# A two-layer model in one program: the state-space loop's order of turn, output and tokens, and one of eight gates computed inside that loop

## The reference, cut to what matters

```
decay = exp(-exp(w)) * (0.5 + 0.5 * tf)          # per batch and channel
ek, ekv = exp(min(f, 30)), exp(min(f, 30)) * f
nf, df  = forward scans of ekv, ek; nb, db = backward scans
euk = exp(min(u + f, 30))
num = nf + nb - ekv + euk * f;  den = df + db - ek + euk
gate = sigmoid(x) * num / max(den, 1e-8) * (0.8 + 0.2 * tf)

x = x + attention(gate0(x))      # 16 heads, causal
x = x + ternary_ffn(gate1(x))
x = x + state_space(gate2(x))    # 64 heads of 8, state 128, chunks of 32
x = x + moe(gate3(x))            # 8 experts, top 2
```

## Time and profile before

| | us |
|---|---|
| median of 3 runs | 716.97 (716.85 to 722.58) |
| the profiled execution, its own time | 719.14 |
| its span | 717.3 |
| PE busy | 557.5 (78%) |
| DVE busy | 405.2 (56%) |
| ACT busy | 370.4 (52%) |
| POOL busy | 147.3 (21%) |

### The profile page before, as it was taken

The page is one execution under the profiler, slowest core; times in us unless marked ns, Lnnn a source line. Parts: engine busy times, 40 slices in busy tenths (PEclk is TensorE's granted clock), DMA queues, the critical chain, the costliest instruction groups (busy, mean ns, idle before and its releaser), DMA issues.

```text
span 717.3 us, 13912 instructions
## 1 busy us (share of the span) xinstructions
PE 557.5 (78%) x5668; PEld 403.4 (56%) x5668; DVE 405.2 (56%) x597; ACT 370.4 (52%) x791; POOL 147.3 (21%) x115
## 2 busy tenths in 40 slices
PE   0187868577967686668999999998639999999980
PEld 0044546454545571345564556666528999997560
DVE  5889998868899367883755545453461121111223
ACT  6986887457786615754557555644321222222212
POOL 1000000000000125841009555520010322322210
PEclk9995687785597999988999999998758999999996
DMA  9500000000000100000000000000049999889825
GB/s 354 163 1 1 1 1 1 1 0 1 1 1 1 30 1 1 0 1 1 1 3 2 2 3 2 3 2 2 31 164 383 422 419 379 307 329 339 309 124 190
DMA packets 18479, 71.38 MB, mean 100 GB/s; under 512 B 4848, under 2 KB 9968, under 8 KB 14704
## 3 DMA queue, kind: packets, MB, share of 16 engines
q1 hardware_dynamic: 15408, 64.20, 23.6%
q0 software_dynamic: 1920, 5.25, 2.0%
q10 hardware_dynamic: 1088, 1.05, 0.4%
HBM read 65.77 MB, written 4.72 MB: 98 GB/s over the span
## 4 chain that ended last, share of the span: by engine, by line
PE 56%; DVE 26%; ACT 10%; issue 4%; DMA 2%; POOL 1%; SPq 0%; ACTq 0%; DVEq 0%; POOLq 0%
PE PS L1416 41%; DVE nmx L1017 3%; DVE arena L930 3%; DVE arena L927 3%; PE PS L1891 2%; PE PS L1454 2%; PE PS L1960 2%; ACT arena L604 1%; PE PS L1667 1%; DVE A L949 1%; PE PS L1532 1%; ACT arena L764 1%; DVE arena L1121 1%; PE PS L1492 1%; DMA arena<-ypair 1%
## 5 line engine op out<-in xcount | busy, mean ns | idle before, releaser
L1416 PE MATMUL PS<-arena 128*128 128x128 f32 (+6 forms) x1376 | 162.1, 296 | 17.1 <-DVE arena L1121 10.1
L1416 PEld LDWEIGHTS PS<-arena 128*128 128x128 f32 (+4 forms) x1376 | 129.3, 167 | 43.0 <-issue 26.1
L604 ACT ACTIVATE arena<-PS,nmx 128x128 f32<-128x128 f32 (+1 forms) x128 | 52.1, 424 | 44.8 <-DVE nmx L1017 44.8
L1469 PE MATMUL PS<-ident,arena 128*128 128x128 f32 x192 | 37.6, 350 | 32.6 <-ACT arena L591 30.5
L1364 DVE TENSOR_TENSOR R<-arena,PS 128x128 f32<-128x128 f32 x16 | 4.6, 288 | 89.3 <-ACT arena L858 89.2
L1469 PEld LDWEIGHTS PS<-ident,arena 128*128 128x128 f32 x192 | 29.1, 181 | 40.4 <-ACT arena L604 25.7
L383 POOL TENSOR_SCALAR arena<-ident,gcol 128x128 f32<-128x128 f32 x4 | 2.4, 601 | 234.0 <-DMA gcol<-in_gcol 234.0
L443 POOL TENSOR_TENSOR arena<-arena 128x1024 f32<-128x1024 f32 x16 | 37.8, 2367 | 41.1 <-DVE arena L1203 33.1
L475 POOL DMA_INDIRECT ypair<-arena,oid x20 | 19.8, 988 | 122.5 <-ACT arena L864 122.5
L1416 PE MATMUL PS<-arena,R 128*128 128x256 f32 x192 | 44.2, 380 | 0.6 <-ACT arena L864 0.6
L1416 PEld LDWEIGHTS PS<-arena,R 128*128 128x128 f32 x192 | 35.2, 190 | 5.1 <-issue 1.0
(11 more groups left out here) (299 smaller groups left out, 1202.9 us busy)
## 6 DMA issues: line engine op xcount, KB each, us to landing
arena<-in_moe SPq DMA_DIRECT2D x23, 1408.0 KB, 6.6
arena<-in_moe SPq DMA_DIRECT2D x23, 768.0 KB
inproj<-in_inproj SPq DMA_DIRECT2D x1, 1344.0 KB, 10.5
arena<-in_fT SPq DMA_DIRECT2D x1, 1024.0 KB, 4.9
xT<-in_xT SPq DMA_DIRECT2D x1, 1024.0 KB, 5.4
R<-in_w1T SPq DMA_DIRECT2D x1, 1024.0 KB, 7.4
R<-in_w2T SPq DMA_DIRECT2D x1, 1024.0 KB, 9.4
R<-in_w3T SPq DMA_DIRECT2D x1, 1024.0 KB, 11.5
```

Source lines behind the costliest of these rows:

```text
L604: sc.activation(pr[u % 2][:, j, 0:n], PS[:, 2 * (u % 2) + j // 2, (j % 2) * 256:(j % 2) * 256 + n], ACT.Exp, bias=nmx[:, u % 2, j:j + 1], ...
L1416: last = mm(dst, l, r, start=(n == 0), stop=(n == len(pairs) - 1))
L1469: last = nc.tensor.transpose(PSB[:, 4 * HALF + c:4 * HALF + c + P], pr[u % 2][:, j, k * P:(k + 1) * P], ident[:])
```

## The change

Three things are changed together.

First, the eighth gate (i = 7, that is m = 3, c = 1, used by the experts' half 1) leaves the attention. FRAME becomes 6 and GATES 7, so that six gates fill the 36 pieces of the attention. The pieces of a gate are cut differently: a scan pair is no longer one piece. k = 1 is now the forward scan alone, and the new k = 7 and k = 8 are the fix of the ends and the backward scan. The pieces of a frame on DVE are now: close the denominator and forward scan of the numerator; backward scan of the numerator; close the numerator; Newton and result; forward scan of the next denominator; backward scan of the next denominator.

Second, the eighth gate is computed in four units t of 256 columns (one channel tile, one batch) inside the state-space loop. SP loads the unit's part of f again. ACT makes its inputs (`unit_inputs`, four instructions) after `by_chunk` of odd tiles and the reciprocal guess (`unit_guess`, three instructions) in even tiles. DVE runs `unit_out(t-1)` and `unit_den(t)` after `gated` in even tiles, and `unit_num(t)` and `unit_min(t+1)` in odd ones, so 7 or 8 instructions in each tile. The decay is now a broadcast column and not a matrix.

Third, the loop's order. On PE, `segments(i+1, 0)` and `(i+1, 1)` stand ahead of `state(i, 1)`, `turn(i-1)` comes right behind `state(i, 1)`, `output(i-1)` behind `state(i, 3)`, and `tokens(i+1)` right ahead of `within(i)`. ACT and DVE follow: `add_out(i-1)` now comes in DVE's turn i, one earlier than before.

```diff
@@ SP @@
-            sp.wait_ge(S["dve_R"], 8)
-            sp.wait_ge(S["act_euk"], 16)
+            sp.wait_ge(S["dve_R"], 7)
+            sp.wait_ge(S["act_euk"], 14)
...
+            sp.wait_ge(S["dve_num"], GATES)
+            for t in range(UNITS):
+                c, ct, n, cols = unit_of(t)
+                if t:
+                    sp.wait_ge(S["act_euk"], 2 * GATES + 3 * t)
+                load(uf[t % 2], a["fT"][:, c, cols], "f")
@@ ACT, attention @@
-                if k == 0 and i < 7:
-                    scaled_inputs(i + 1, 0)
-                if k == 4 and i < 7:
-                    scaled_inputs(i + 1, 1)
                 if k == 1:
                     reciprocal_guess(i)
-                if k == 2 and i < 7:
-                    decay(i + 1)
-                if k == 3 and i < 7:
-                    bonus(i + 1)
+                if i < GATES - 1:
+                    if k == 2:
+                        decay(i + 1)
+                    if k == 3:
+                        scaled_inputs(i + 1, 0)
+                        bonus(i + 1)
+                    if k == 4:
+                        scaled_inputs(i + 1, 1)
@@ ACT, loop @@
+            def unit_inputs(t):
...
+                done(sc.activation(uek, uek, ACT.Exp))
+                sc.activation(uxe, uek, ACT.Copy, scale=dq[:, 3, ct, n:n + 1]).then_inc(S["act_euk"], 1)
+                sc.activation(ufc, uf[t % 2], ACT.Copy, scale=cb[:, n:n + 1]).then_inc(S["act_euk"], 1)
+                sc.activation(ug, uf[t % 2], ACT.Exp, bias=wu[:, 3, 1, ct:ct + 1]).then_inc(S["act_euk"], 1)
...
             by_chunk(0)
+            unit_inputs(0)
             for i in range(NT):
-                state(i, 1)
                 if i + 1 < NT:
                     decays(i + 1, 0)
                     decays(i + 1, 1)
+                state(i, 1)
+                if i:
+                    turned(i - 1)
                 state(i, 2)
                 state(i, 3)
+                if i % 2 == 0:
+                    unit_guess(i // 2)
+                if i:
+                    inverse_root(i - 1)
...
-                if i:
-                    turned(i - 1)
-                    inverse_root(i - 1)
+                if i % 2 and i < NT - 1:
+                    unit_inputs(i // 2 + 1)
@@ DVE @@
-                for part in ((0,), (2,), (3,), (5, 6), ())[k]:
+                for part in ((0, 2), (8,), (3,), (5, 6), (), ())[k]:
                     gate_step(i, part)
...
-                if k == 4 and i < 7:
-                    gate_step(i + 1, 1)
+                if k >= 4 and i < GATES - 1:
+                    gate_step(i + 1, 1 if k == 4 else 7)
...
+            def unit_scan(t, x, y):
+                c, ct, n, cols = unit_of(t)
+                d = dec[:, 3, ct, n:n + 1].broadcast_to([P, T])
+                done(v.tensor_tensor_scan(y, d, x, 0.0, ALU.mult, ALU.add))
+                done(v.tensor_tensor(y[:, T - 1:T], y[:, T - 1:T], rdq[:, 3, ct, n:n + 1], ALU.mult))
+                done(v.tensor_tensor_scan(y[:, 0:T - 1][:, ::-1], d[:, 1:T], y[:, 0:T - 1][:, ::-1], y[:, T - 1:T], ALU.mult, ALU.add))
...
             for i in range(NT):
                 if i:
                     gated(i - 1)
-                if i >= 2:
-                    add_out(i - 2)
+                if i % 2 == 0:
+                    if i:
+                        unit_out(i // 2 - 1)
+                    unit_den(i // 2)
+                else:
+                    unit_num(i // 2)
+                    if i < NT - 1:
+                        unit_min(i // 2 + 1)
+                if i:
+                    add_out(i - 1)
                 if i + 1 < NT:
                     front(i + 1)
             gate(3, 0)
             gated(NT - 1)
-            add_out(NT - 2)
+            unit_out(UNITS - 1)
@@ PE, loop @@
             for i in range(NT):
-                state(i, 1)
                 if i + 1 < NT:
                     segments(i + 1, 0)
                     segments(i + 1, 1)
-                    tokens(i + 1)
+                state(i, 1)
+                if i:
+                    turn(i - 1)
                 state(i, 2)
                 state(i, 3)
+                if i:
+                    output(i - 1)
                 if i + 1 < NT:
                     segments(i + 1, 2)
                     segments(i + 1, 3)
                 if i % 2 == 0:
                     state(i, 4)
+                if i + 1 < NT:
+                    tokens(i + 1)
                 within(i)
-                if i:
-                    turn(i - 1)
                 between(i)
-                if i:
-                    output(i - 1)
@@ tables @@
-FRAME = 5
+FRAME = 6
+GATES = 7
+UNITS = 4
```

More of the change, by code:

```diff
@@ L138, in build, with unit_of @@
         wter = arena[:, 27 * K:30 * K].bitcast(BF).rearrange("p (w n) -> p w n", w=3)
+        uf = [ekvq[:, 512 + T * i:512 + T * (i + 1)] for i in range(2)]
+        uek, ufc, uxe, uxv = [dmats[0][:, T * i:T * (i + 1)] for i in range(4)]
+        ug, unf, udf, udb = [dmats[1][:, T * i:T * (i + 1)] for i in range(4)]
+        def unit_of(t):
+            c, ct, b = 1, t // 2, t % 2
+            n = 2 * c + b
+            return c, ct, n, slice(ct * HALF + b * T, ct * HALF + (b + 1) * T)
         def by_half(o):
@@ L973, in _ @@
             gate_step(0, 1)
+            gate_step(0, 7)
             gate_step(0, 0)
             gate_step(0, 2)
+            gate_step(0, 8)
             gate_step(0, 3)
@@ L982, in _ @@
             gate_step(1, 1)
+            gate_step(1, 7)
             def ternary(w):
```

57 lines of the change are left out of this document (44 added, 13 removed).

## The result

The changed kernel takes 727.74 us (median of 4 runs, 726.89 to 729.61), the kernel before 716.91 (four runs now, 716.16 to 722.58). The ratio, taken over the runs and not from the two medians, is 1.0137, 95% interval 1.009 to 1.0184. The forecast was 715.8, no change; the time lies in its wide range of 702 to 733, but 10.8 us of loss were measured and 1.1 of gain forecast. Now and then a run of any kernel takes a slower course, and the ratios leave such runs out where enough others are left. The profiled execution has a span of 726.5 us against 717.3.

The account below looks back on a forecast made before the run. The prediction took DVE as the fullest engine in the attention (PE too at the low clock) and PE as full in the state-space loop. 716.97 - 15 (attention) + 13.8 (loop) = 715.8 us, 8-in-10 range 702 to 733.

Parts of the forecast that it names:

- The attention, -15: Attention: one gate fewer takes some 17 us off DVE; -15 us on the path, between -8 and -20.
- The first half: Attention up to the second half's first maxima: 12.05 us gained, those maxima near 153.
- one of the signs named for being wrong: Attention, units 8 to 11: a DVE wait on PE that does not go would show the forecast wrong.
- The second half: Attention, units 16 to 27: gains of 0.3, 1 and 4 us, less 2.5 for ACT's heavier pieces.
- The port: Loop, tiles 2 and 4: POOL's steps holds gated's two-SBUF-input instruction on DVE; PE waits 3.7, 6.65 us lost per tile.
- The waits of the loop as a sum: Loop: waits and slow stretches behind them come to 24.05 us after, against 10.25 before.
- slow stretches only behind two waits: Loop: low clock costs 2.95 us behind the waits in tiles 2 and 4, and no longer in tile 7.
- small pieces in place of 2.97 + 2.95: Loop, tile 7: waits of 2.75 us in small pieces replace a 2.97 us wait and its 2.95 us slow stretch.
- A: Main case: attention and loop as worked out, port holding gated in tiles 2 and 4; 715.8 us, chance 0.40.
- B: Rival, loop: the port does not hold gated, so the loop costs only +1.3; 703 us, chance 0.32.
- D: Rival, attention: it gives only 8 us because PE bounds it at the low clock; 723 us, chance 0.08.
- C: Rival, loop tiles 1, 3, 5: POOL keeps the port between instructions, 19.7 us more; 735.5 us, chance 0.20.

Follow-up runs that it names:

- e1: Changed kernel with the loop's order of before and no units, so the eighth gate is not computed: 706.94 us, ratio 0.9847 to the kernel before.
- e18: Changed kernel, old loop order, units behind addition to x, first unit ahead, late sigmoid, 16 extra products, ACT's next-gate work in three pieces: 704.43 us.
- e5: Changed kernel without units (no eighth gate), POOL's steps held until gated is done: 715.33 us; loop 144.86 us, for 158.72 without that wait.
- e12: Kernel before plus only 40 small extra products, read by nobody, in TensorE's idle start: 725.81 us, ratio 1.01.

## Why the prediction was wrong

**The attention, -15.** Measured -13.3 at its last addition, with a start 0.5 us later; the other profiled executions with the same attention had -9 to -14, at a granted clock between 0.62 (e1) and 0.73 from 50 to 100 us, so the term is good to no more than 2 or 3 us. The first half was right as a sum: from its first maxima to those of the second half it takes 102.6 us for 116.0, 13.4 less, where 12.05 was forecast, and the second half's first maxima come at 151.99 for "near 153". By groups this is luck in part. Units 4 to 7 gave 3.0 us for 1, units 8 to 11 gave 2.1 for 4.5 (DVE's wait on PE behind them stayed, 2.04 us for 2.16, one of the signs named for being wrong), and the rest up to the second half's first maxima 8.3 for 6.55. The second half failed: 83.67 us for 84.12, so 0.45 us of the 5.3 less 2.5; units 20 to 23 lost 1.6 where 1 was to be gained, and units 24 to 27 gave 1.8 of 4. PE waits 1.74, 2.20 and 1.98 us for ACT's copies (L607) in the long group that I took for bound by PE at the low clock. The cause stays open, since e18 rules out only the spread of ACT's work. The loop's first segment came at 364.00, for "near 365"; that figure was at odds with the forecast itself, whose -15 puts it near 362 (376.71 before).

**The port, the mechanism that decided.** Right in kind, place and nearly in size. L1277 takes 2.66 and 2.90 us in tiles 2 and 4 ("near 2.5"; the mean of all four is 1.61, since two do not meet steps), PE waits 2.62 and 2.85 ("some 3.7"), and with the slow rows behind the waits tiles 2 and 4 cost 7.0 us each, for 6.65; here a wait forecast 1.0 us too long and a slow stretch 1.3 us too short nearly cancelled. Without the conflict they would cost 1.0 on the forecast's account, 11.3 less in both; e5 gave 13.9. The Trainium skill (SBUF — State Buffer, Who interferes with whom) says that the later of the two engines waits for the whole instruction of the other. The rows shown here agree, 2.66 us for 0.56 in tile 2.

**The waits of the loop as a sum.** Forecast 18.15 us of standing after (24.05 less two slow stretches of 2.95) against 7.3 before, +10.85. Measured 23.4 against 12.5 (either with 5.2 us ahead of the second router product, which the forecast left out of both), +10.9. That is luck in part: three waits put down to issue, 3.15 us, weren't in it, while tiles 2 and 4 waited 1.9 us less than forecast, and tile 0, tile 6 and the end 1.3 less.

**The step that failed: slow stretches only behind two waits.** The forecast gave the low clock to tiles 2 and 4 and took it away from tile 7: 2 x 2.95 - 2.95, +2.95 us. Measured is +11.6 of busy time. Slow rows added 8.6 us in tiles 2 and 4 instead of 5.9. And tiles 0 and 1, the last tile and what follows it had slow stretches as well, each behind waits that I had priced at their own length alone. Against the same rows at the upper clock I estimate 1.5, 1.6, 3.3 and 1.1 us for them; with the 8.6, less the 2.95 of before, that is 1.5 us more than the 11.6 measured, so they are rough. One of these stretches, the output products in tile 7:

```profile
499.46:504.52 5.06, 5.06 (x25) 4.93 (x24) 0.00 (x0) 0.60 (x1) 0.00 (x0) 0.53 0.01 3
```

That stretch of tile 7 stands behind waits of 0.94, 1.27 and 0.63 us. I called them "small pieces in place of 2.97 + 2.95" and so struck out a slow stretch that stayed. Between the two profiled executions the miss is 10.4 us: +9.2 for -1.2, the -15 and +13.8 of the forecast. Of it 8.7 are this term, 2.3 the attention's as it stood at the loop's start and 0.1 the waits; 0.7 came back behind the loop.

**The chances.** A had 0.40 and its mechanism was the real one, but 727.74 lies outside its own range of 709 to 722. The outcome "slower", above 724.1, had 0.27, less than "within" with 0.38. B, which needed a port that does not hold `gated`, falls by L1277 alone, and D by the attention's 13.3 us. C's place was wrong (L1271 took 0.86 us in tile 1, not over 3), and a loss of 10.8 us for its 18.5 came by another way.

## What to carry to other kernels

Before an engine's result is brought one place nearer to its reader, look at which long instruction of the port's other user stands beside it then: one wait on the other engine was worth 13.9 us here. The sum of the waits was only half the price in this loop, in which PE was full; ask of each wait what clock the rows behind it have. And before a difference of 1 per cent is called an effect of an edit, shift the same kernel's TensorE instructions by a part of a block (here 160 of some 252) and time it again.

## What the hardware showed that was not expected

- **A block of instructions.** 160 instructions in idle time at the start made both orders slower, the kernel before by 1.0 per cent (1.0066 to 1.0134); 64 instructions made it no slower (0.9973), 256 gave the old picture. The single waits are 0.2 to 2.0 us, and each ends 2.2 to 2.9 us after a transfer of instructions has begun.
- **Two engines at one port.** At the border of two POOL instructions DVE's waiting one went first (0.86 us in tile 1, for 0.84 in tile 7, where it also waits for masked_decay and no steps follows), and POOL's next is put down as begun but is 0.3 us longer.
- **Not every wait brings the low clock.** Behind the waits of 1.94 and 1.85 us in e12 the granted clock stayed at 1.00 (394 to 400 and 486 to 497 us); behind 0.94, 1.27 and 0.63 us in the changed kernel it fell to 0.53, and in e5 rows of 2.18 us took 2.98 behind waits of only 0.60 and 0.41. No run here tells what decides.
